# The first pair of a two-batch-element pipeline: order of chunk and output weight loads, and of ScalarE's quantisations

## The reference

```
x = x + fake_quant(layernorm(x)) @ fake_quant(ctx)          # 8 bit codes, scale and zero point
x = x + attention(layernorm(x))                             # qkv_w 1024x3072, 32 heads of 32, rope, causal, out_w 1024x1024
x = x + ffn(layernorm(x))                                   # x @ W.T + bias, and 16 experts of rank 16 added up
fake_quant(v) = (clip(round(v / s + z), 0, 255) - z) * s
```

## Time and profile before

| | us |
|---|---|
| median of three runs | 644.33 (643.79 to 645.38) |
| the profiled execution | 645.53 |
| its span, first to last instruction | 643.9 |
| TensorE busy in it | 604.1 |
| VectorE busy | 448.6 |
| ScalarE busy | 297.6 |
| mean granted TensorE clock | 0.986 |

### The profile page before, as it was taken

The page is one execution under the profiler, slowest core; times in us unless marked ns, Lnnn a source line. Parts: engine busy times, 40 slices in busy tenths (PEclk is TensorE's granted clock), DMA queues, the critical chain, the costliest instruction groups (busy, mean ns, idle before and its releaser), DMA issues.

```text
span 643.9 us, 12627 instructions
## 1 busy us (share of the span) xinstructions
PE 604.1 (94%) x4832; PEld 299.6 (47%) x4832; DVE 448.6 (70%) x897; ACT 297.6 (46%) x374; POOL 11.1 (2%) x20
## 2 busy tenths in 40 slices
PE   1669987999999999999999999999999999899997
PEld 0234442454545555554445455544544554354453
DVE  7599995779747854885586568537865569767661
ACT  5888765774455545545634554555331233101010
POOL 3000000000000000000000000000000000000000
PEclk9879999999999999999999999999999999899999
DMA  9999896862284156317712751463240062023221
GB/s 320 385 388 383 331 301 235 280 227 70 98 263 164 67 195 213 115 65 259 258 69 84 251 186 65 168 219 103 98 163 2 1 212 97 35 78 119 84 79 49
DMA packets 38878, 109.17 MB, mean 170 GB/s; under 512 B 4026, under 2 KB 4282, under 8 KB 38848
## 3 DMA queue, kind: packets, MB, share of 16 engines
q1 hardware_dynamic: 37072, 104.35, 46.3%
q0 software_dynamic: 1344, 4.23, 1.7%
q10 hardware_dynamic: 432, 0.18, 0.1%
HBM read 100.35 MB, written 8.39 MB: 169 GB/s over the span
## 4 chain that ended last, share of the span: by engine, by line
PE 81%; DVE 11%; DMA 3%; SPq 2%; ACT 1%; issue 1%; DVEq 0%; ACTq 0%
PE dense L1104 16%; PE dense L1106 15%; PE dense L1105 15%; PE cross L1141 7%; PE turn L1095 6%; DVE wq L774 4%; PE dense L1235 4%; PE dense L1236 4%; PE dense L1237 4%; PE score L1198 2%; SPq L532 2%; DMA wq<-in_ctx 2%; PE score L1222 2%; DMA lnt<-in_ctx 1%; PE dense L1117 1%
## 5 line engine op out<-in xcount | busy, mean ns | idle before, releaser
L1104 PE MATMUL dense<-wq,xn_h 128*128 128x512 f16 x400 | 152.4, 381 | 0.0
L1105 PE MATMUL dense<-wq,xn_h 128*128 128x512 f16 x400 | 151.9, 380 | 0.0
L1106 PE MATMUL dense<-wq,xn_l 128*128 128x512 f16 x400 | 151.9, 380 | 0.0
L318 ACT ACTIVATE code<-raw,cst,qc 128x1024 uint8<-128x1024 f32 x74 | 90.2, 1237 | 17.9 <-DMA raw<-in_ctx 17.1
L1141 PE MATMUL cross<-code,q1t 128*128 128x512 f16 x256 | 74.7, 393 | 8.5 <-ACT code L318 4.2
L1106 PEld LDWEIGHTS dense<-wq,xn_l 128*128 128x128 f16 x400 | 39.2, 98 | 47.5 <-issue 0.6
L1104 PEld LDWEIGHTS dense<-wq,xn_h 128*128 128x128 f16 x400 | 39.2, 98 | 40.8 <-issue 2.8
L1105 PEld LDWEIGHTS dense<-wq,xn_h 128*128 128x128 f16 x400 | 39.3, 98 | 37.8 <-issue 0.9
L334 ACT ACTIVATE at<-turn 128x512 f32<-128x512 f32 x32 | 19.1, 597 | 76.8 <-PE turn L1095 76.0
L318 ACT ACTIVATE code<-lnt,cst,qc 128x1024 uint8<-128x1024 f32 x34 | 42.1, 1238 | 26.9 <-DMA lnt<-in_ctx 19.9
L803 DVE TENSOR_REDUCE smx<-score 128x8 f32<-128x512 f32 x32 | 22.0, 686 | 44.0 <-PE score L1198 44.0
(11 more groups left out here) (159 smaller groups left out, 935.8 us busy)
## 6 DMA issues: line engine op xcount, KB each, us to landing
raw<-in_ctx SPq DMA_DIRECT2D x74, 512.0 KB, 4.8
lnt<-in_ctx SPq DMA_DIRECT2D x34, 512.0 KB, 4.3
wo<-in_ctx SPq DMA_DIRECT2D x12, 512.0 KB, 9.1
wo<-in_qkv_w SPq DMA_DIRECT2D x12, 512.0 KB, 12.3
wq<-in_ctx SPq DMA_DIRECT2D x8, 512.0 KB, 11.5
wq<-in_qkv_w SPq DMA_DIRECT2D x8, 512.0 KB, 12.1
x_scratch<-xb SPq DMA_DIRECT2D x8, 512.0 KB, 3.2
wq<-x_scratch SPq DMA_DIRECT2D x8, 512.0 KB, 3.7
```

The lines of the kernel that those rows point to most:

```text
L318: act.activation(low_bytes, src, ACT.Identity, scale=qc[:, 1:2], bias=z2).then_inc(s_u8, 1)
L1104: pe.matmul(bank[:, :], a_h[:, k, :], w_hi, start=(k == 0 and not started), stop=False)
L1105: pe.matmul(bank[:, :], a_h[:, k, :], w_lo, start=False, stop=False)
L1106: ins = pe.matmul(bank[:, :], a_l[:, k, :], w_hi, start=False, stop=(k == KC - 1 and not last))
```

## The change

On ScalarE chunks 8 and 9 of pair 1 are quantised right behind chunk 7, ahead of the first `p_evac`; chunk 10 ahead of `c_whole(0)`; chunks 11 to 14 are spread anew; chunk 15 behind `c_whole(1)` where it was ahead of it. On SP's queue W27 and W28 go ahead of W24 to W26, and chunks 10 to 15 follow without weights in between.

```diff
                 exponent(0, 1)
-                q(5, 6, 7)
+                q(5, 6, 7, 8, 9)
                 p_evac(0, 0)
                 v_evac(0, 0)
-                q(8)
                 p_evac(0, 1)
                 exponent(0, 2)
                 exponent(0, 3)
+                q(10)
                 c_whole(0)
                 v_evac(0, 1)
-                q(9, 10, 11)
+                q(11, 12)
                 p_evac(0, 2)
-                q(12)
+                q(13)
                 p_evac(0, 3)
-                q(13, 14, 15)
+                q(14)
                 c_whole(1)
+                q(15)
                 w(24)
...
-            for j in range(W_QKV, W_QKV + 3):
+            for j in (27, 28, 24, 25, 26):
                 load_weight(j)
-            load_chunk(1, 10)
-            load_chunk(1, 11)
-            load_weight(27)
-            load_chunk(1, 12)
-            load_chunk(1, 13)
-            load_weight(28)
-            load_chunk(1, 14)
-            load_chunk(1, 15)
+            for c in range(10, CHUNKS):
+                load_chunk(1, c)
             for j in range(29, W_ALL):
                 load_weight(j)
```

## The result

| | before | after |
|---|---|---|
| median of 11 runs each | 645.31 us (643.14 to 647.00) | 648.75 us (645.78 to 650.40) |
| ratio after / before, 95% interval | | 1.0051 (1.0033 to 1.0070) |
| profiled execution: its time, its span, mean granted clock | 645.5, 643.9, 0.986 | 650.4, 648.8, 0.976 |

The forecast was 645.3 us in a range from 643.7 to 647.2, most likely no measurable difference. The kernel is slower by more than the 0.3% that a measurement tells, and its time lies outside the range. (The 11 runs before include the three of the table ahead of the prediction, whose median is 644.33.)

The account below looks back on a forecast made before the run. When TensorE starts chunk 15 (101.65) was taken to decide the first pair's end, with TensorE busy without a break from 120 us. Projection 1.42 late less 0.41 gained: +1.0 on 644.33, 645.3 us; range 643.7 to 647.2.

Parts of the forecast that it names:

- Chunks 8 and 9 early: ScalarE quantises them right behind chunk 7; the probability tile is delayed by 0.1 us and caught up: cost 0.
- Chunk 10 on the path: Ahead of c_whole(0): it lands at 87.5, so TensorE's output projection starts at 89.43 instead of 88.01, 1.42 us late.
- The moved loads: SP's queue: W27 and W28 put 1.05 MB more in front of chunk 10; 1.6 us per load, landing at 87.5.
- that estimate: Chunk 10's landing from the 358 GB/s limit: 1.46 us per load, landing at 86.7, not late; sum 0.3 us.
- Chunk 15 behind c_whole(1): TensorE starts chunk 15 13.23 us behind the projection's start, against 13.64 now: a gain of 0.41 us.
- W29 to W31: Weight loads following chunk 15's load, at about 92; no longer hold projection tiles 5 to 7: 0.
- The sum: Projection 1.42 us late less 0.41 gained at chunk 15: +1.0 us on 644.33, giving 645.3.
- rival 1: The longer pause ahead of the projection drops TensorE's clock to half: +1.0 + 1.5, 646.8; chance 0.30.
- Everything behind the turns follows it at a fixed distance: End of the first pair: the time TensorE starts chunk 15, now 101.65, decides everything behind the turns.
- Rival 3: The longer pause ahead of the turns hides the half clock of 111 to 114: -0.7, 643.6; chance 0.08.
- Rival 2: The DMA hole takes both moved loads and chunk 10 isn't late: +0.3, 644.6; chance 0.15.
- The fall of the clock between 88 and 94 us: TensorE's granted clock falling there was one of the signs named as proving the forecast wrong.

Follow-up runs that it names:

- e2: The kernel before with ScalarE's new order alone, SP's loads as before: 648.57 us, ratio 1.0062 to before.
- e3: The kernel before with SP's new load order alone, ScalarE's list as before: 644.13 us, ratio 0.9976 to before.
- e1: The changed kernel with chunk 10 put back behind the first context evacuation and the value copy: 645.68 us, ratio 1.0020 to before.
- e4: The changed kernel with eight dummy matmuls in TensorE's pause ahead of the projection: 646.82 us, ratio 1.0033 to before.
- e11: The changed kernel with chunk 15 alone put back ahead of the second context evacuation: 646.09 us, ratio 1.0019 to before.
- e6: The kernel before with ten dummy matmuls in TensorE's pause ahead of the turns: 646.02 us, ratio 1.0023 to before.
- e9: The kernel before with one unused activation more on ScalarE ahead of c_whole(0): 646.12 us, ratio 1.0026 to before.
- e5: The changed kernel with eight dummy matmuls ahead of the projection and 14 ahead of the turns: 645.57 us, ratio 1.0013 to before.
- e10: The kernel before with one unused activation ahead of c_whole(0) and eight dummy matmuls in the pause there: 646.89 us, ratio 1.0028 to before.

## Why the prediction was wrong

**Chunks 8 and 9 early: right.** Cost 0. The probability tile starts at 83.07 and the exponential at 86.51, later than before only by what the execution already had.

**Chunk 10 on the path: right, its landing by luck.** The forecast landing was 87.5, measured 87.67 with 0.26 of shift. But chunk 9 landed at 79.2 (issued at 72.2, 7.0 us), not at 77.9. The moved loads aren't the reason: the same load took 7.0 us in e2, which has the loads of before, and 6.0 in e3, which has the new ones. It varies by execution. The six loads behind it then took 8.5 us, 1.41 each, not 1.6. The Trainium skill ("DMA: Bandwidth & Descriptors", Specifications) gives about 358 GB/s, an estimated 1.46 us per load; the trace nearly agrees with that spacing, but 6 x 0.524 MB in 8.5 us is 371 GB/s, more than the page's limit. What failed in that estimate was its start, a landing that one execution had shown. The projection was 1.29 us late, forecast 1.42.

**Chunk 15 behind c_whole(1): right.** 13.24 us behind the projection in e1 and in e4, at full clock, forecast 13.23; 1.34 us of wait for ScalarE, and no load in it. W29 to W31 showed in no wait.

**The sum: the failing step.** "Sum. 1.42 - 0.41 = +1.0 us" took the work behind the projection at full clock. I did name the mechanism that broke it, as rival 1, with a chance of 0.30, and weighed the pause by its length against the 2.57 us that I had seen. Two things were wrong with that. I held the 0.85 us of work between two pauses to be a protection; the profiles of after and e11 show the half clock after 1.26 idle, 0.85 of small matmuls and 2.1 idle, and 7 of 11 runs of after have a mean clock of 0.981 or less. And I priced one stretch, 3.4 us long: it was 6.8 long, and the one at the turns had doubled as well. Why isn't shown: that pause grew from 2.57 to 3.83 us, but behind one of 3.83 the stretch lasted 3.4 us in e1, e2 and e4. The rival's +1.5 measured 2.7 + 1.0 in the profiled execution, and with it failed "Everything behind the turns follows it at a fixed distance" (7.08 us to the next stage, before 6.06). A third thing I did not see: the early loads take away TensorE's waits ahead of chunks 13 to 15. In e6 and e9 these waits took up most of a slow and half of a late projection; in after and e11 they are gone, and a slower TensorE comes through in full (2.7 us).

**Rival 3** failed: the half clock of the turns began in the longer pause, at about 112.1 with the turns at 113.40, but it got longer too. **Rival 2**: chunk 10 was late. The fall of the clock between 88 and 94 us was named as what would prove the forecast wrong, and it did.

Shown: the loss hangs on ScalarE's order (e2, e3), on chunk 10's and chunk 15's places about equally (e1, e11), and in the profiled execution 3.75 of 4.89 us of it are clock. That the empty pause brings low clocks is shown by how often they stand in the runs with it and without (after, e2, e9, e11 against e4, e5, e10). Open: where and how often the half clock falls in the runs that weren't profiled is known only through mean clocks; filling a pause restores the clock but not all of the time (e4, e10); and why dummy matmuls cost 0.4 to 1.2 us at 570 us.

## What to carry to other kernels

Before an optional job goes ahead of an evacuation that TensorE waits for, ask two things: has its data landed by then, and does TensorE work without a break behind the pause? If it does, price the pause at the half clock that may follow (up to 6.8 us at half here), not at its idle time, and not by a single profiled execution: sort the runs by mean granted clock, and look in the profile for falls that have nothing to do with the change. A schedule that leaves TensorE no waits behind the pause turns a slow stretch into lost time in full: 2.7 us in after, against 0.5 in e6, which still had waits.

## What the runs showed of the hardware

- After two pauses with 0.85 us of small matmuls between them, the granted clock fell to half in the profiles of after and e11 (second pause 2.08 and 2.05 us) and stayed full in those of e2 and e9 (1.60 and 1.69 us). In e6 it fell with a second pause of 0.80 us, behind which it stayed full in the kernel before. Runs of one kernel differ by 4 us with it (646.3 at a mean clock of 0.986, 650.1 at 0.976). The stretches at half in the two main profiles lasted from 3.4 to 6.8 us.
- A half clock can cost little: at the turns of the kernel before it mostly hides loads (e6), and behind the projection in e6 waits took up 1.2 of 1.7 us. Near 551 us it cost its full 1.7 us.
- One and the same load of 512 KB (chunk 9) took from 6.0 to 7.0 us to land in the fourteen profiles (6.0 in before, e3 and e8, 7.0 in after, e2 and e4). An argument that hangs on tenths of a landing needs more than one profile.
